# A graph network's third layer: how many tiles go by dense rows, how many by gathered neighbours

## The reference

```python
h = relu(layernorm(x)); x = x + L0(h, adj)   # inv_deg * (adj @ h + beta*h) @ kernel + bias
h = relu(layernorm(x)); x = x + L1(h, adj)   # softmax over neighbours of adj*score, times h
h = relu(layernorm(x)); x = x + L2(h, adj)   # relu([h, adj @ h] @ W.T + b)
h = relu(layernorm(x)); x = x + L3(h, adj)   # four attention heads over neighbours, gated
```

## Time and profile before

| | us |
|---|---|
| median of 3 runs | 1193.59 |
| lowest, highest | 1185.4, 1194.25 |
| the profiled execution | 1189.68 |
| its span from first to last instruction | 1188.0 |
| mean granted TensorE clock | 0.85 of full speed |

### The profile page before, as it was taken

How to read it: one execution, slowest core, us unless ns; L and a number is a source line. 1 busy time by engine, 2 the same in 40 slices (tenths; PEclk the granted TensorE clock), 3 DMA queues, 4 the chain that set the end, 5 groups by cost and what they waited for, 6 DMA issues and landing times.

```text
span 1188.0 us, 25534 instructions
## 1 busy us (share of the span) xinstructions
PE 895.1 (75%) x5768; PEld 569.3 (48%) x5768; DVE 822.4 (69%) x2230; ACT 687.1 (58%) x3070; POOL 509.9 (43%) x526
## 2 busy tenths in 40 slices
PE   4979999999999352666667469997667788888750
PEld 1535555556455221555556334554444555555540
DVE  7388879879788774666665761121655888888788
ACT  4999879987977031434433351000455778888762
POOL 4002767735333434555555401666214444444420
PEclk9999988988989575676665679998897999999985
DMA  9556657657450125444444538984233444444421
GB/s 367 192 207 244 241 205 290 231 203 262 170 188 27 54 86 169 133 134 134 127 121 119 179 109 343 356 290 116 89 126 111 121 116 119 120 123 122 119 72 71
DMA packets 109354, 196.19 MB, mean 165 GB/s; under 512 B 21152, under 2 KB 93088, under 8 KB 103488
## 3 DMA queue, kind: packets, MB, share of 16 engines
q1 hardware_dynamic: 84368, 74.10, 19.8%
q10 hardware_dynamic: 8448, 82.99, 18.0%
q0 software_dynamic: 16432, 37.97, 11.7%
HBM read 166.17 MB, written 25.97 MB: 162 GB/s over the span
## 4 chain that ended last, share of the span: by engine, by line
PE 42%; DVE 22%; issue 17%; ACT 7%; another core or an unknown queue 2%; DVEq 2%; SPq 1%; DMA 1%; POOL 1%; ACTq 0%; POOLq 0%
PE ps L1877 7%; PE ps L1768 7%; PE ps L1852 4%; ACT unread L936 4%; PE ps L1931 4%; DVE work L1265 4%; PE ps L1922 3%; DVE work L1575 3%; PE ps L1794 2%; PE ps L1836 2%; DVE work L1266 2%; PE ps L1720 2%; PE ps L1716 2%; PE ps L1845 1%
## 5 line engine op out<-in xcount | busy, mean ns | idle before, releaser
L936 ACT ACTIVATE unread<-work 128x128 bf16<-128x128 f32 x1024 | 300.7, 295 | 6.9 <-ACT unread L936 2.1
L1768 PE MATMUL ps<-work,h_wide 128*128 128x512 f32 x512 | 241.8, 629 | 17.3 <-ACT h_wide L848 17.3
L936 ACT ACTIVATION_READ_ACCUMULATOR unread<-work 128x1 f32 x1024 | 191.6, 187 | 0.0
L755 POOL DMA_INDIRECT work<-in_adj_rows,adj_stage x120 | 157.3, 1311 | 60.1 <-issue 32.9
L1768 PEld LDWEIGHTS ps<-work,h_wide 128*128 128x128 f32 x512 | 101.3, 203 | 140.3 <-issue 138.6
L797 POOL DMA_INDIRECT work<-h_table,stage x105 | 100.2, 954 | 126.7 <-DMA h_table<-h_wide 59.3
L797 POOL DMA_INDIRECT work<-kv_table,node_flat x93 | 89.1, 958 | 121.7 <-PE ps L1941 77.5
L1575 DVE CUSTOM_DVE_ANT_0 work<-ps,work 128x512 f32<-128x512 f32 x168 | 116.2, 747 | 22.0 <-PE ps L1922 20.0
L1931 PE MATMUL ps<-ident,work 128*128 128x128 f32 x648 | 95.9, 281 | 42.6 <-issue 22.6
L1029 ACT ACTIVATE work<-work 128x512 f32<-128x512 f32 x165 | 117.2, 713 | 11.9 <-DVE work L1584 7.8
L797 POOL DMA_INDIRECT work<-h_table,node_flat x93 | 88.5, 951 | 71.8 <-issue 38.6
(11 more groups left out here) (230 smaller groups left out, 1655.7 us busy)
## 6 DMA issues: line engine op xcount, KB each, us to landing
work<-in_adj_rows ACTq DMA_DIRECT2D x38, 2048.0 KB
work<-adj_table SPq DMA_DIRECT2D x66, 192.0 KB
work<-in_adj_rows SPq DMA_DIRECT2D x6, 2048.0 KB
mask_table<-work SPq DMA_DIRECT2D x43, 128.0 KB
work<-mask_table SPq DMA_DIRECT2D x43, 128.0 KB
work<-kv_table SPq DMA_DIRECT2D x43, 128.0 KB
adj_table<-work SPq DMA_DIRECT2D x42, 128.0 KB
work<-in_adj_rows SPq DMA_DIRECT2D x66, 64.0 KB
```

Of the source, the lines that this page charges most:

```text
L755: nc.gpsimd.indirect_dma_start(out=ag[:, h, c, :], out_offset=None, in_=adj_rows, in_offset=bass.IndirectOffsetOnAxis(ap=adj_stage[:, h // ...
L936: ins = nc.scalar.activation(unread[:, m % (MQ // 2) * TB + t, :], ring[:, q, m, t * P:(t + 1) * P], ACT.Abs, accum_out=seen[:, b, t, q * ...
L1768: ins = mm(ps[:, 0, :], h_sb[:, q * MQ + m, :], ring[:, q, m, :], start=(q + m == 0), stop=False)
```

## The change

The number of dense blocks falls from three to two, so tiles 8 to 11 become gathered tiles: 8 dense, 24 gathered. FIXED follows (it becomes 5, so 20 groups are written out), and EACH is set to 2 dense products a group, which fills 16 of the 20. Block 1 is now turned and added within the groups, behind group 17, and there is nothing in `between`. On ACT, the issue of pieces 2 and 3 of block 0, and with it of all pieces behind them, waits for all stored rows, and the copy of the last dense sum comes ahead of the square root for the first eight tiles (`deviations`).

```diff
-DB = 3
+DB = 2
 DT = DB * TB
 FIXED = (T - DT) // NBUF2 - 1
 PLAIN = T // NBUF - 1
 EARLY = 4 * MQ
-EACH = (DB * T - EARLY) // (FIXED * NBUF2)
+EACH = 2
...
             act.wait_ge(slot_full[1], 16 * (NB + 1))
+            for b in range(TB):
+                act.wait_ge(row_stored[b], rows_of_before(3))
             settle(act)
             for s in range(2, DB * NQ):
...
                 if nb and q == NQ - 1:
                     dense_out(nb - 1)
+            dense_out(DB - 1)
             deviations(3, slice(LAST_GROUPS[0], LAST_GROUPS[1]))
-            dense_out(DB - 1)
...
             def dense_added(j):
-                for nb in range(DB - 1):
+                for nb in range(DB):
                     if j == quad_of_unit(T * nb + T - 1) + 2:
                         add_block(nb)
...
-            sparse_quads(dve, step2, dense_added, lambda: add_block(DB - 1))
-            dve.wait_ge(dense_read, DB)
+            sparse_quads(dve, step2, dense_added)
...
             def dense_part(j):
-                for nb in range(DB - 1):
+                for nb in range(DB):
                     if j == quad_of_unit(T * nb + T - 1) + 2:
                         turn_block(nb)
-                for n in range(EACH):
-                    dense(EARLY + EACH * j + n)
+                for u in range(EARLY + EACH * j, min(DB * T, EARLY + EACH * j + EACH)):
+                    dense(u)
...
-            last = sparse_quads(pe, neighbours, dense_part, lambda: turn_block(DB - 1))
+            last = sparse_quads(pe, neighbours, dense_part)
```

## The result

The changed kernel took **1221.76 us** (median of four runs, 1219.36 to 1234.68) for 1193.61 us: ratio **1.0274, interval 1.0202 to 1.0346**, 28 us slower. Forecast was 1203 us, within 1186 to 1216: right sign, less than half the size. The profiled execution took 1234.68 us, 13 us over its median, and block 0 begins in it at 727.81 us, 8.4 us later than the 719.39 of the earlier trace rows, though the kernel is unchanged up to there. So I compare by distance from block 0's first product, and call the distance from there to layer four's first gather **S**. Before, S was 885.00 − 719.39 = 165.6 us; after, it is 927.53 − 727.81 = 199.7 us. That is 34.1 us more, for 28 us by the medians: one profile says where time goes better than how much of it.

What follows compares the result with a forecast made beforehand. It took TensorE and GpSimd's gathers as nearly in balance, the gathers slower. Terms +11.5 + 0 + 0.5 gave +12 us on this execution's 1189.7, 1201.7; forecast 1203 us, range 1186 to 1216.

Steps and rivals of the forecast that it cites:

- Part 3: Start of layer three's gathers: rows stored earlier, quads 0 to 3 fetched by 740, quad 4's gather 3.1 us earlier.
- part 6: Block 0's pieces 2 and 3, issued later on ACT: cost between 0 and 3 us, taken as +0.5 us.
- Part 4: GpSimd's pace for quads 4 to 23: between 3.75 and 4.55 us a quad, last gather later by +11.5 us.
- Part 5: Tail into layer four keeps its length, 0; block 1's turn and add lie beside waiting, 0, else 0.5 us.
- Parts 1 and 2: Layer three: 32 dense products less save TensorE 27.7 us; four more gathered quads cost GpSimd 15.0 us of gathers.
- A: GpSimd's runs in layer three: kept-back notices and pauses stay, +9 to +16 us; the forecast case, chance 0.58.
- B: GpSimd from the first run after 748.9: gathers run on without pause, −9 to +5 us; chance 0.26.
- C: TensorE in groups 0 to 15: its low clock becomes the bound, +15 to +25 us; chance 0.10.
- D: Start of gathers: rows not earlier, or pieces 2 and 3 hold up block 0; +3 us on A; chance 0.06.

Runs made afterwards that it cites:

- e1: Changed kernel, but ACT no longer waits for the stored rows before issuing pieces 2 and 3 of block 0: 1218.86 us, ratio 1.0231.
- e3: Changed kernel with VectorE's add of block 1, its residual, statistics and moments behind group 19 in place of 17: 1222.05 us, ratio 1.0245.
- e4: Changed kernel with both edits, no store wait on ACT and block 1 added behind group 19: 1212.68 us, ratio 1.0177.
- e12: Changed kernel once more, on a chip where the kernel before takes 1132 to 1136 us: 1149.98 us, ratio 1.0125.
- e16: Changed kernel again (two blocks, with the store wait), on a chip where the kernel before takes 1132 to 1136 us: ratio 1.0130.
- e14: Changed kernel without the store wait (two blocks), on a chip where the kernel before takes 1132 to 1136 us: ratio 1.0052.
- e7: Kernel of e4 with two gathers a quad in layer three in place of three (result partly wrong): 1191.45 us, ratio 0.9867.
- e8: Kernel before, groups beginning after two dense pieces in place of four, pieces 2 to 4 held for landed rows, no padding gathers: 1202.7 us, ratio 1.0042.
- e11: Kernel before, ACT waiting for stored rows before piece 2 and quad 2's landed rows before piece 4, no padding gathers: ratio 1.0074.
- e2: Kernel before with one edit alone, ACT waiting for the stored rows before pieces 2 and 3: 1209.84 us, ratio 1.0160.
- e6: Kernel of e4 with one 128x16 memset on GpSimd behind each quad's three gathers: 1219.55 us, ratio 1.0106.
- e10: Kernel of e4 with ten small chained memsets on GpSimd after every second quad's gathers: ratio 1.0304.

## Why the prediction was wrong

Against block 0's start, the last padding gather ended at 118.8 us before and 147.6 after: +28.8 for the 11.5 forecast. From there to layer four's first gather it took 46.8 us before and 52.1 after: +5.3 for 0. Together these are the 34.1 us of S; 28 us is the change of the medians.

- **Part 3, where the gathers begin, is the step that failed.** Rows stored early, the first gather at 3.5 us: right. "Quads 0 to 3 fetched by 740" was wrong: GpSimd issued their gathers by 746, and quad 0's rows landed at 767. I priced pieces 2 and 3 by their own landing (part 6, +0.5 us; block 0 took 27.73 us as before, so that cost was 0) and let the small loads pass as if the queues were free, though the stretch that I had read shows a DMA share of 1.02. Quad 4's gather was 9.8 us late where −3.1 stood: 12.9 us of the sum in the profiles. By the times of the two-block kernel the wait costs less, 2.9 (e1) and 9.4 us (e3 and e4), and e12, e16 and e14 have it at 0.7 to 0.8%; with three blocks it cost 1.60% and 1.16%. With the bytes of block 1 gone, the changed kernel stood at 1.0031 for 1.0125 and 1.0130.
- **Part 4, the pace**: 20 quads of kept-back notices. From quad 4's gather to the padding 94.3 us, for 75.2 before: +19.1, where 14.6 was taken (11.5 net of the 3.1). e3, e1 and e4 had 90.3, 92.3 and 92.5: +15 to +17, near the forecast. The runs of twelve (17.84 us, 4.46 us a quad, for 4.40) were foreseen; shorter runs and the long pause between them were not. Mechanism right, size a little short.
- **Part 5, "beside waiting: 0"**: in the profiled execution block 1's add cost 6.2 us on VectorE, ahead of the indices of the next quad, since it waits for a notice kept back. It is a place that the change itself moved into the groups, and its 6.2 us are within the pace above. By the times (e3, e4) it is not shown. The tail, taken as 0, grew by 5.3 us: TensorE's first projection of layer four followed the end of the last padding gather by 4.2 us, where it stood 5.3 us before it in the kernel before, for the last add now came behind the padding. e3 and e4 show the same (52.5 and 52.3 us), e1 does not (46.6), and on the other chips the tail is 41 to 44 us with either kernel. What decides it stays open.
- **Parts 1 and 2** were right: TensorE has slack, the four quads cost gathers. Without the wait they cost 5.3 us of S where notices come at once, and 18.0 (e1) and 23.0 (e4) where they don't.
- **Rivals.** A's mechanism was at work on the chip of the forecast; by the profile, the 12.9 us that part 3 missed took the time out of its range and of mine. B, gathers without a pause, is what happens on the other chips, and even there the change is 1.3% slower, with the store wait taken out 0.5%, the top end of B's −9 to +5. C, the clock: it fell to the low level behind each wait of some 5 us (quad 2.05 us, products 3.03 for 1.88) and was back by the next group 4.7 us on; granted 0.92 and 0.82 in the groups. What I weighed from the Trainium skill (TensorE: Matmul & The Clock Gate, HAM oscillation), that repeated waits bring the clock down again and again, agrees with this trace, but the gathers set the time and not the groups (e7). D's second half, pieces in the way, was the right place and had 0.06; I gave it +3 us, and looked there for block 0's pieces to be late and not for the rows. The sign came out right by part 4: without the wait the change is slower too (e1, e4, e14).

## What to carry to other kernels

Before moving large transfers behind or before small ones, count what each queue holds at that moment. Here, with a DMA share near 1, the small loads landed only as the large ones ran out, 31.8 us after they were asked for. So request the rows that the next step needs before the pieces that it doesn't, or keep few large pieces in flight. A wait added to order two transfers also starts everything behind it together. Holding pieces back did not make the kernel before faster (e8, e11). And read a pace from several chips, or leave room for it: half of this change's cost was there on one kind of chip only.

## What the runs showed of the hardware

- On some chips (kernel before 1192 to 1205 us), notices of TensorE to VectorE, ACT, GpSimd and SP that fell into a long run of indirect gathers came mostly 2 to 3 us after its end; on others (1132 to 1136 us) as a rule within 0.2 us of the product, with the same kernel and the same 0.94 us a gather. On the first kind they too came within 0.2 us where GpSimd ran three gathers and stopped (e2, e8), while 0.3 us between gathers, with or without a memset, was no such stop (e6). What makes the chips differ stays open, and a break put in on purpose was tried only on a chip that does not need it (e10).
- Three queues with work in all of them moved 223, 224 and 223 packets in 10 us, of 15, 2 and 0.7 KB on average: alike by the packet, and not by the byte.
- A 128x16 memset on GpSimd (0.13 us) is free between two indirect gathers, which start 1.25 us apart for 0.95 us of work (e6).
